# A fused attention and feed-forward block on one core: another opening, and other orders of work in the main loop

## Chip, core and metric

One core of a Trainium2 chip runs the whole program as one launch. The metric is the device time in microseconds (us), lower is better. The times of the kernel before are the median of three runs; the profile is of one further execution.

## What is computed

The input x has 4 sequences of 1024 tokens of width 256, all float32. The reference, cut to what matters:

```python
xn = layernorm(x)                                   # per token, over 256
q = rope(xn @ wq + bq) * 16 ** -0.5                 # 16 heads of 16
k = rope(xn @ wk + bk); v = xn @ wv + bv            # 2 groups of 16; 8 query heads share a group
attn = softmax(q @ k.T * 16 ** -0.5)                # per head, 1024 x 1024
att = (attn @ v).reshape(4, 1024, 256) @ wo + bo
hidden = silu(xn @ W1.T) * (xn @ W3.T)              # width 1024
hidden = fwht(hidden)                               # Walsh-Hadamard transform over 1024, / sqrt(1024)
out = x + att + hidden @ W2.T
```

The transform over `hidden` is put onto `W2` once, in the opening: a transform over 1024 is one over 8 (between chunks of 128) times one over 128 (within a chunk, a product with a 128x128 matrix `had`).

## The kernel before

**Blocks and iterations.** The 4096 tokens are 8 blocks of 512 (`NBLK`). There are 8 iterations (`NIT`), one for each sequence and group of heads. An iteration `i` computes the attention of 8 heads over a whole sequence, and in its gaps it prepares block `i + 2` and computes the feed-forward part of block `i`.

**Periods.** An iteration has 16 periods. Each has two steps `j`. A step has four score products on TensorE (`score`, L1374), four exponentials on ScalarE (L942) and one accumulation of exponentials times values (`sums`, L1387). Each period also holds four units `S1` of a first pass over the scores (L1297), whose maxima VectorE takes (`unit`, L1124); this pass runs 24 units ahead (`LEAD`), since the second pass subtracts the maxima inside its product.

**Fillers.** `main_entry` and `extra_entry` say what else a period holds: `XT` turns a normalised block (L1313), `QK` and `Q2` project queries, and keys and values (L1277), `VT` turns values, `MT` turns maxima (L1302), `WO` applies wo (L1307), `UP` makes one eighth of the hidden layer (L1339), `DN` applies W2 (L1352), `W2` does the 128-wide part of the transform of the weights (L1359). Before, iteration 0 has `XT`, `QK`, `W2`, `W2` in periods 0 to 3, then eight `UP` and four `DN`. Iterations 1 to 5 have `XT`, `QK`, `WO`, `WO`, eight `UP`, four `DN`. Iterations 6 and 7 have nothing in periods 0 and 1. A kind with an `MT` or `VT` beside it has an x behind its name (`UPx`).

**The ring.** All but the second-pass scores and the sums share two PSUM slots of two banks. `piece` waits until its slot has been emptied by ScalarE, VectorE or both. The order of the pieces on TensorE within a period is written out by hand for each kind in `walk_iteration`; `own` issues pieces of the filler, `first` an S1 unit, `scores` a pair of score products. ScalarE's, VectorE's and GpSimd's orders are written out by hand too, and each engine works strictly in its order.

**Second pass.** Its scores use three PSUM banks in turn: product `u` waits for exponential `u - 3`.

**The opening** (`walk_opening`) has two blocks: loads, statistics on VectorE, `root` (L805 to L811) on GpSimd, `normalise` (L886) on ScalarE, transposes, projections, rotation of queries (`rotate_queries`, L548 to L562) and keys (`rotate_keys`, L572 to L579), a way through HBM that changes the layout (`store_queries`, `store_keys`, `load_keys`, `load_queries`), and 24 S1 units. The 8-wide part of the transform of W2 is `transform`, three stages of two operations each (L526, L527), two stages on VectorE and one on GpSimd. `weights_lo` (L532) splits the first weights. Products of 32-bit values are made as three products of a high and a low part (`TERMS`), except the transposes, `WO`, `W2` and the sums, which are plain float32.

## Time and profile before

| what | value |
|---|---|
| median of 3 runs | 1179.03 us (1177.75 to 1181.44) |
| profiled execution, its own time | 1181.6 us |
| its span, first to last instruction | 1179.8 us |
| TensorE busy | 1049.8 us, 89% |
| VectorE, ScalarE, GpSimd busy | 783.2, 704.7, 352.2 us |
| mean granted TensorE clock | 0.936 of full speed |
| start of the first exponential | 100.90 us |

Views name the engines PE (TensorE), PEld (its weight loads), DVE (VectorE), ACT (ScalarE), POOL (GpSimd) and SP (SyncE); a q behind a name is the engine's queue, which issues DMAs. A row of the timeline has the start in us, the duration of the merged group, the engine, the line, the operation and its tiles, the count, and in brackets the idle time of the engine before it and what ended it.

### The profile page before, as it was taken

The numbers are of one execution on the slowest core, as the hardware profiler recorded it, in microseconds if no ns is written. First come the engines' busy times: TensorE is split into PE (matmuls) and PEld (weight loads), VectorE is DVE, ScalarE is ACT, GpSimd is POOL, SyncE is SP. The second block draws the span as 40 slices with busy tenths as digits, with TensorE's granted clock in tenths as the row PEclk, the third lists the DMA queues.
The fourth block names the chain that finished last, engine by engine and source line by source line (L and its number), as shares of the span: only waits on it lengthen the run. The fifth ranks groups of instructions, "written<-read, shape, count | busy, mean of one in ns | idle before, by whom it ended". The sixth has DMA issues, their size and how long they took to land.

```text
span 1179.8 us, 19333 instructions
## 1 busy us (share of the span) xinstructions
PE 1049.8 (89%) x7584; PEld 547.5 (46%) x7584; DVE 783.2 (66%) x891; ACT 704.7 (60%) x1318; POOL 352.2 (30%) x299
## 2 busy tenths in 40 slices
PE   0358899989998999989998999989999999999994
PEld 0314354544555455544555445554445344544552
DVE  4895477757776577766777577765777777687611
ACT  2204377656765477655775567754775667656771
POOL 1652523107330254106330164204440023102310
PEclk9755799989999899989999799989999999999997
DMA  8247022412314223412205123421204101410001
GB/s 222 67 150 192 21 67 68 101 59 72 89 31 88 70 82 88 94 63 75 83 13 109 54 99 89 88 69 31 73 20 101 48 24 46 95 36 6 7 17 51
DMA packets 62732, 84.27 MB, mean 71 GB/s; under 512 B 16688, under 2 KB 31920, under 8 KB 62640
## 3 DMA queue, kind: packets, MB, share of 16 engines
q1 hardware_dynamic: 59328, 78.30, 24.8%
q10 hardware_dynamic: 3312, 4.72, 1.6%
q8 instruction: 60, 0.98, 0.4%
q14 instruction: 32, 0.26, 0.1%
HBM read 55.18 MB, written 22.54 MB: 66 GB/s over the span
## 4 chain that ended last, share of the span: by engine, by line
PE 79%; DVE 12%; ACT 3%; issue 2%; ACTq 1%; SPq 1%; DMA 1%; POOL 0%; POOLq 0%; DVEq 0%
PE ps L1387 19%; PE ps L1339 16%; PE ps L1374 15%; PE ps L1297 13%; DVE negpart L1124 9%; PE ps L1352 7%; PE ps L1277 3%; PE ps L1307 3%; ACT work L942 2%; PE ps L1313 1%; ACTq L878 1%; DVE y L1106 1%; PE ps L1302 0%; DVE y L1104 0%; ACT osum L950 0%
## 5 line engine op out<-in xcount | busy, mean ns | idle before, releaser
L1124 DVE TENSOR_REDUCE negpart<-ps 128x2 f32<-128x1024 f32 x512 | 619.3, 1223 | 272.6 <-PE ps L1297 267.7
L942 ACT ACTIVATE work<-ps 128x512 f32<-128x512 f32 x1024 | 552.9, 605 | 266.4 <-PE ps L1374 211.0
L1297 PE MATMUL ps<-kb,qh 48*128 48x512 f32 x1024 | 257.7, 472 | 53.4 <-DVE negpart L1124 27.4
L1374 PE MATMUL ps<-qh,kb 50*128 50x512 f32 x1024 | 272.0, 470 | 20.0 <-ACT work L942 19.3
L1387 PE MATMUL ps<-work,vb 128*32 128x512 f32 x2048 | 282.0, 626 | 0.0
L1374 PEld LDWEIGHTS ps<-qh,kb 50*128 50x128 f32 x1024 | 121.2, 192 | 218.9 <-ACT work L942 166.8
L1339 PE MATMUL ps<-xf,w_p 64*128 64x512 f32 x1536 | 207.1, 401 | 5.9 <-DVE negpart L1124 3.5
L1297 PEld LDWEIGHTS ps<-kb,qh 48*128 48x128 f32 x1024 | 109.2, 197 | 149.0 <-DVE negpart L1124 83.2
L1339 PEld LDWEIGHTS ps<-xf,w_p 64*128 64x128 f32 x1536 | 140.7, 186 | 52.6 <-DVE hid L1096 12.7
L825 POOL TENSOR_TENSOR hid_p<-hid,hid_p 128x512 fp32r<-128x512 f32 x64 | 82.3, 1286 | 196.0 <-ACT hid_p L933 196.0
L831 POOL TENSOR_TENSOR attnt<-attnt,recips 128x512 f32<-128x512 f32 x16 | 20.4, 1278 | 374.6 <-DMA recips<-recip_rows 374.6
L821 POOL TENSOR_TENSOR hid<-hid 128x512 f32<-128x512 f32 x64 | 82.4, 1288 | 150.8 <-DVE hid L1096 147.5
L1352 PE MATMUL ps<-w2t_p,hid_p 64*128 64x256 f32 x1536 | 114.5, 279 | 0.0
L1352 PEld LDWEIGHTS ps<-w2t_p,hid_p 64*128 64x128 f32 x1536 | 110.1, 185 | 5.6 <-DVE negpart L1124 1.4
L1387 PEld LDWEIGHTS ps<-work,vb 128*32 128x32 f32 x2048 | 41.4, 109 | 83.1 <-issue 57.6
L921 ACT ACTIVATE hid<-ps 128x512 f32<-128x512 f32 x64 | 38.6, 603 | 42.5 <-PE ps L1339 41.0
L1104 DVE TENSOR_TENSOR y<-y,ps 128x256 f32<-128x256 f32 x32 | 13.4, 419 | 59.0 <-PE ps L1352 59.0
L1307 PE MATMUL ps<-wo_sb,attnt 128*128 128x256 f32 x128 | 40.6, 429 | 12.5 <-POOL attnt L831 12.5
L1096 DVE SCALAR_TENSOR_TENSOR hid<-hid,ps 128x512 f32<-128x512 f32 x64 | 43.4, 678 | 9.4 <-ACT hid L921 9.4
L886 ACT ACTIVATE xn<-xn,nmr,rstd 128x256 f32<-128x256 f32 x28 | 15.0, 596 | 43.7 <-POOL nmr L811 43.6
L933 ACT CAST hid_p<-hid 128x512 fp32r<-128x512 f32 x64 | 40.3, 630 | 0.0
L1277 PE MATMUL ps<-xt,wqkv_p 128*128 128x512 f32 x126 | 37.4, 446 | 1.6 <-ACT qe L908 0.9
(109 smaller groups left out, 489.0 us busy)
## 6 DMA issues: line engine op xcount, KB each, us to landing
xf<-xn_parts SPq DMA_DIRECT2D x32, 512.0 KB, 7.8
qh<-qk_parts SPq DMA_DIRECT2D x192, 64.0 KB, 2.2
xn_parts<-xt SPq DMA_DIRECT2D x14, 512.0 KB, 3.6
y<-in_x SPq DMA_DIRECT2D x8, 512.0 KB, 4.1
attnt<-osum SPq DMA_DIRECT2D x128, 32.0 KB, 2.0
recips<-recip_rows SPq DMA_DIRECT2D x128, 32.0 KB, 1.8
out<-y SPq DMA_DIRECT2D x8, 512.0 KB, 2.9
xn<-in_x SPq DMA_DIRECT2D x7, 512.0 KB, 4.5
```

The costliest lines, as they stand in the source:

```text
L821: nc.gpsimd.tensor_tensor(hid[1][:, c, :], hid[1][:, c, :], hid[0][:, c, :], ALU.mult).then_inc(hid_done, 1)
L825: nc.gpsimd.tensor_tensor(hid_p[1][:, c, :], hid[1][:, c, :], hid_p[0][:, c, :].bitcast(F32), ALU.subtract).then_inc(hid_lo, 1)
L942: nc.scalar.activation(prob[j % 2][:, h, :], ps[:, 4 + u % 3, :], ACT.Exp, scale=SCALE).then_inc(exp_done, 1)
L1096: nc.vector.scalar_tensor_tensor(at, at, 1.0, two(slot)[:, 0, :], ALU.add, ALU.mult).then_inc(ring_free[slot], 1)
L1124: nc.vector.tensor_reduce(negpart[a][:, f, :, h, t, e], two(slot), AX.X, ALU.max, negate=True).then_inc(ring_free[slot], 1)
L1277: m = pe.matmul(out, left[a], right[b], start=(first and n == 0), stop=(last and n == 2))
L1297: m = pe.matmul(bank[:, r, :], qh[2 * q + f][rows, h, t * P:(t + 1) * P], kb[i % 2][rows, e * 512:(e + 1) * 512], start=True, stop=True)
L1307: m = pe.matmul(bank[:, k // 2, k % 2 * D:(k % 2 + 1) * D], attnt[:, f, k * P:(k + 1) * P], wo_sb[:, i % NG, :], start=True, stop=True)
L1339: m = pe.matmul(bank[:, r, :], w13_p[w][rows, k, c * P:(c + 1) * P], xf[v][rows, k, :], start=(k == 0 and t == 0), stop=(done and t == 2))
L1352: m = pe.matmul(bank[:, r, 0:D], hid_p[w][rows, c, at * P:(at + 1) * P], w2t_p[v][rows, c, :], start=(c == 0 and t == 0), stop=(c == HC - ...
L1374: pe.matmul(ps[:, 4 + u % 3, :], kb[i % 2][rows, kt * P:(kt + 1) * P], qh[2 * a + f][rows, h, :], start=True, stop=True).then_inc(s2_done, 1)
L1387: m = pe.matmul(ps[VW * h:VW * (h + 1), 7, :], vb[b % 2][g][:, kt, :], prob[j % 2][:, h, :], start=(kt == 0), stop=(kt == ST - 1))
```

## The change

**Opening.** The first weights (`w13_raw`), `bo` and `wo` are no longer loaded from ScalarE's queue at the start, but from SyncE's after the queries of iteration 0. W2 and `had` are loaded from SyncE's queue. Six of VectorE's ten initial memsets go to GpSimd (two small zeros, four of ones in `kb`). ScalarE casts `wqkv` first, then normalises both blocks. TensorE's order is by kind, both blocks each: `XT`, `Q2`, `QK`, `VT`. VectorE rotates the keys of both blocks and then the queries of both; GpSimd rotates none. Keys are stored and loaded back from ScalarE's queue.

**W2.** Of the three stages of the 8-wide transform, one is left (on GpSimd). The other two and the 128-wide part are one accumulation on TensorE, `weights2`, 32 products of 128x128 by 128x256 in float32, between `VT` and the first S1 unit, in the four banks that the second pass uses later. The `W2` fillers are gone.

**Turned block.** Its evacuation is done in two halves (`turned_hi(m, k)`, `turned_lo(m, k)`).

**Placement.** Iteration 0 has nothing in periods 0 and 1, `XT` and `QK` in 2 and 3; the cast of the first weights (`weights_hi`) and the normalisation of block 2 stand on ScalarE at the end of periods 0 and 1, and `weights_lo` is all on GpSimd. In iterations 6 and 7 `WO` is in periods 0 and 4, `UP` in 1, 2, 3, 5, 6, 7, 8, 10, and 9 and 11 have no filler.

**Orders.** Nearly all hand-written orders within a period differ. The core of the diff:

```diff
+def turn_at(i):
+    return 0 if i > 0 else 2
+def sums_at(i):
+    return (2, 3) if i + 2 < NBLK else (0, 4)
+def up_at(i):
+    return range(4, 12) if i + 2 < NBLK else (1, 2, 3, 5, 6, 7, 8, 10)
...
+FULLS = {"XT": 2, "QK": 2}
+FREES = {"XT": 2, "UP": 2, "VT": 2}
...
         elif kind == "XT":
-            sums_before()
-            own(0)
-            first(1)
-            extra()
-            first(1)
-            scores(0)
-            own(1)
-            scores(1)
-            first(1)
-            scores(2)
-            first(0)
-            scores(3)
-            sums(i, 2 * p)
+            first(1)
+            own(0, 1)
+            scores(0)
+            scores(1)
+            sums_before()
+            extra()
+            first(0)
+            first(1)
+            scores(2)
+            scores(3)
+            first(0)
+            sums(i, 2 * p)
...
         elif kind == "UPx":
+            scores(0)
             first(0)
-            scores(0)
+            first(1)
             sums_before()
             scores(1)
-            first(1)
-            own(0, 1)
-            first(1)
-            own(2, 3)
-            first(1)
+            own(0)
             scores(2)
+            first(1)
+            own(1, 2)
+            first(1)
+            own(3)
...
         elif kind == "WO":
+            extra()
+            first(0)
+            first(0)
+            sums_before()
+            first(1)
+            scores(0)
+            scores(1)
+            own(0, 1, 2, 3)
...
-def walk_opening(piece):
-    for entry, slot in ((("XT", 0), 0), (("XT", 1), 1), (("QK", 0), 0), (("Q2", 0), 0), (("QK", 1), 1), (("Q2", 1), 0),
-                        (("VT", 0), 1), (("VT", 1), 0)):
-        for k in range(PIECES[entry[0]]):
-            piece(entry, k, slot)
+def walk_opening(piece, weights2):
+    for kind in ("XT", "Q2", "QK", "VT"):
+        for m in range(2):
+            for k in range(PIECES[kind]):
+                piece((kind, m), k, m)
+    weights2()
...
@@ SyncE @@
             load_tables(1)
+            sp.dma_start(w2h[0], w2t.rearrange("(c p) n -> p c n", p=P)).then_inc(w2_in, 16)
+            sp.dma_start(had, had_in).then_inc(w2_in, 16)
             swap_keys(0)
             swap_keys(1)
             store_queries(0)
-            store_keys(0)
-            store_keys(1)
-            load_keys(0)
             load_queries(0, 0, 0)
...
             place_maxima(0, 0, 0)
-            load_turned(0)
             load_queries(0, 1, 0)
             load_queries(0, 1, 1)
+            for n in range(2):
+                cols = slice(n * HID // 2, (n + 1) * HID // 2)
+                for r, src in enumerate((w1t, w3t)):
+                    sp.dma_start(w13_raw[GRP * r:GRP * (r + 1), :, cols],
+                                 src.rearrange("(c p) n -> p c n", p=GRP)[:, :, cols]).then_inc(w13_in[n], 16)
+            sp.dma_start(bo_sb[:, :], bo.partition_broadcast(P)).then_inc(bo_in, 16)
+            sp.dma_start(wo_sb[:, :, :], wo.rearrange("(g p) n -> p g n", p=P)).then_inc(wo_in, 16)
+            load_turned(0)
...
@@ GpSimd @@
             root(1)
-            rotate_keys(pool, nc.gpsimd, 0)
-            rotate_queries(pool, nc.gpsimd, 1)
-            weights_lo(pool, nc.gpsimd, 1)
-            transform(pool, nc.gpsimd, 1)
+            pool.wait_ge(w2_in, 32)
+            pairs = [t.rearrange("p (n s) d -> p n s d", s=2) for t in w2h]
+            for n, op in enumerate((ALU.add, ALU.subtract)):
+                nc.gpsimd.tensor_tensor(pairs[1][:, :, n, :], pairs[0][:, :, 0, :], pairs[0][:, :, 1, :],
+                                        op).then_inc(w2h_done, 1)
             root(2)
+            for n in range(2):
+                weights_lo(pool, nc.gpsimd, n)
...
@@ ScalarE, kinds UP and XT @@
                         exponentials(i, j, 1, 4)
+                        gate(i, up_at(i).index(p))
                         hidden_before(i, p)
-                        gate(i, p - 4)
                         exponentials(i, j, 4, 5)
-                        linear(i, p - 4)
+                        linear(i, up_at(i).index(p))
                         exponentials(i, j, 5, 8)
...
                     elif kind == "XT":
-                        turned_hi(i + 2)
+                        turned_hi(i + 2, 0)
+                        exponentials(i, j, 0, 1)
+                        turned_hi(i + 2, 1)
+                        exponentials(i, j, 1, 3)
                         save_finished(i, p)
-                        exponentials(i, j, 0, 8)
+                        exponentials(i, j, 3, 8)
...
@@ TensorE @@
+            def weights2():
+                pe.wait_ge(w2h_done, 2)
+                for o in range(HC):
+                    for c in range(o % 2, HC, 2):
+                        sign = bin(o // 2 & c // 2).count("1") % 2
+                        m = pe.matmul(ps[:, 4 + o // 2, o % 2 * D:(o % 2 + 1) * D], had[:, sign * P:(sign + 1) * P],
+                                      w2h[1][:, c, :], start=(c < 2), stop=(c >= HC - 2))
+                    if o % 4 == 3:
+                        m.then_inc(w2_full, 1)
```

## Rows read from the trace of the kernel before

**Rows 1.** The page's costliest groups: busy us, mean ns, idle before and its releaser.

```profile
L821 POOL TENSOR_TENSOR hid<-hid 128x512 f32<-128x512 f32 x64 | 82.4, 1288 | 150.8 <-DVE hid L1096 147.5
```

**Rows 2.** Windows, one per iteration (0, 1, 2): length, busy (count), clock, DMA.

```profile
100.90:246.80 145.90, 134.36 (x946) 69.94 (x946) 93.79 (x107) 88.96 (x167) 47.38 (x39) 0.91 0.27 74
246.80:380.80 134.00, 127.47 (x946) 66.76 (x946) 93.47 (x108) 87.31 (x166) 43.93 (x38) 0.97 0.28 71
380.80:517.10 136.30, 130.09 (x946) 67.86 (x946) 93.53 (x108) 87.26 (x166) 43.91 (x38) 0.95 0.28 77
```

**Rows 3.** The chain that ended last, within the opening: start, us, what.

```profile
7.92 9.03 ACTq L878
...
59.52 2.08 DMA qh<-qk_parts
...
62.51 18.20 DVE negpart L1124 x16
```

**Rows 4.** Loads issued in the first 30 us: count, KB, median us to landing.

```profile
hid<-in_w3t ACTq DMA_DIRECT2D x2, 512.0 KB, 15.1
...
xn<-in_x SPq DMA_DIRECT2D x1, 512.0 KB, 5.3
attnt<-in_x SPq DMA_DIRECT2D x1, 512.0 KB, 9.8
```

**Rows 5.** Timeline of the opening, all engines.

```profile
23.21 1.40 DVE L1071 BATCH_NORM_STATS2 stats<-attnt 128x6 f32<-128x256 f32 x4
...
27.00 2.07 ACT L886 ACTIVATE attnt<-attnt,nmr,rstd 128x256 f32<-128x256 f32 x4 [2.28 <-POOL nmr L811]
...
30.75 3.66 PE L1277 MATMUL ps<-xt,wqkv_p 128*128 128x512 f32 x12
...
37.79 0.69 DVE L552 TENSOR_TENSOR qe<-qe,tabq_sb 128x512 f32<-128x512 f32 x1
...
46.81 1.63 DVE L575 TENSOR_TENSOR hid<-hid 128x512 f32<-128x512 f32 x1
```

**Rows 6.** Timeline: eight instructions of four float32 products of 256 columns.

```profile
121.75 1.99 PE L1359 MATMUL ps<-y,osum 128*128 128x256 f32 x8
...
1171.28 3.75 PE L1307 MATMUL ps<-wo_sb,attnt 128*128 128x256 f32 x8 [12.51 <-POOL attnt L831]
```

**Rows 7.** Windows before and in stretches of lower clock; columns as in rows 2.

```profile
240.40:247.20 6.80, 4.10 (x31) 1.70 (x23) 4.70 (x5) 1.77 (x3) 0.00 (x0) 0.99 0.20 54
247.20:254.00 6.80, 6.51 (x25) 3.48 (x25) 3.55 (x4) 4.77 (x10) 0.00 (x0) 0.50 0.50 176
...
643.00:649.90 6.90, 5.43 (x45) 2.52 (x41) 4.43 (x5) 1.66 (x4) 0.00 (x0) 1.00 0.22 59
649.90:663.50 13.60, 12.08 (x41) 5.93 (x42) 7.17 (x6) 7.68 (x15) 0.00 (x0) 0.50 0.25 89
...
97.80:114.00 16.20, 15.32 (x51) 7.59 (x52) 8.39 (x7) 7.73 (x14) 4.69 (x2) 0.50 0.73 220
```

**Rows 8.** Timeline of iteration 1's period 0, which turns a block.

```profile
244.07 0.50 PE L1297 MATMUL ps<-kb,qh 48*128 48x512 f32 x2 [1.32 <-DVE negpart L1124]
...
245.43 1.01 ACT L896 CAST xt<-ps 128x1024 fp32r<-128x1024 f32 x1 [5.14 <-PE ps L1313]
...
247.49 0.79 PE L1374 MATMUL ps<-qh,kb 50*128 50x512 f32 x1 [1.67 <-ACT work L942]
```

**Rows 9.** Timeline of a plain UP period, iteration 1.

```profile
291.10 0.62 ACT L933 CAST hid_p<-hid 128x512 fp32r<-128x512 f32 x1
...
291.77 0.60 ACT L921 ACTIVATE hid<-ps 128x512 f32<-128x512 f32 x1
...
292.41 0.60 ACT L942 ACTIVATE work<-ps 128x512 f32<-128x512 f32 x1
```

**Rows 10.** Timeline around the first UP period of iteration 0.

```profile
142.53 2.93 PE L1339 MATMUL ps<-xf,w_p 64*128 64x512 f32 x12 [1.32 <-DVE negpart L1124]
...
146.24 1.93 PE L1387 MATMUL ps<-work,vb 128*32 128x512 f32 x8
```

More of the change, by code:

```diff
@@ L67, in extra_entry @@
 def extra_entry(i, p):
-    if p == 1 and i + 2 < NBLK:
+    if p == turn_at(i) + 1 and i + 2 < NBLK:
         return ("Q2", i + 2), 0
@@ L205, in walk_iteration @@
             scores(1)
+            sums_before()
             scores(2)
+            scores(3)
             first(1)
-            sums_before()
             own(0, 1, 2, 3)
             first(1)
-            scores(3)
+            sums(i, 2 * p)
             extra()
-            sums(i, 2 * p)
         elif kind is None:
@@ L269, in walk_iteration @@
             scores(3)
-        elif kind == "W2x":
+        elif kind == "XTx":
+            first(1)
+            own(0, 1)
+            scores(0)
+            scores(1)
+            sums_before()
+            first(0)
+            first(1)
+            scores(2)
+            scores(3)
+            first(0)
+            sums(i, 2 * p)
+            extra()
+        elif kind == "QKx":
             scores(0)
             first(1)
+            first(0)
+            scores(1)
             sums_before()
-            scores(1)
-            first(1)
-            own(0, 1)
             scores(2)
@@ L317, in skip @@
         pass
-    walk_opening(count)
+    walk_opening(count, skip)
     for i in range(NIT):
@@ L488, in build @@
         N_PARTS = 16 * 8
+        N_QUERIES = 16 * 4
         NORM = 4
@@ L1062, in _ @@
+                    if i == 0 and p < 2:
+                        normalise(2, range(2 * p, 2 * p + 2))
+                        weights_hi(p)
                     if p in (13, 14) and i + 3 < NBLK:
```

460 lines of the change are left out of this document (227 added, 233 removed).

## Prediction

> **What bounds the kernel now.** I read the table of busy times first: TensorE is busy for 89% of the span, far above the others. Then the windows, one per iteration: in iterations 1 and 2 TensorE is busy for 127.5 of 134.0 us and for 130.1 of 136.3 us, while VectorE has 93.5 and ScalarE 87.3 [rows 2]. So from iteration 1 on TensorE sets the pace, and an order within a period can give back only the 6 us or so per iteration in which it idles, and what its clock costs. These two iterations do the same work; the granted clock is 0.97 in the one and 0.95 in the other, which is one stretch of 6.8 us more at half clock (1.2 instead of 2.4 GHz), and that costs 136.3 - 134.0 = 2.3 us. Then the opening: its chain goes through a stalled DMA issue on ScalarE (9.03 us), projections, rotations, the way through HBM, and 1.14 us per S1 unit on VectorE (18.20 / 16) [rows 3]. The first exponential is at 100.90 us, and TensorE hardly works until then. This is where there is something to gain. The end isn't touched.
>
> **The opening, step by step.** The stalled issue goes, since ScalarE has four loads left. Block 1 is now the late one: it is the third issue of SyncE, near 1.8 us, and lands 9.8 us later [rows 4], at 11.6; bounds are 5.3 us (block 0's) and 9.8. Statistics to normalisation took 27.00 - 23.21 = 3.8 us, normalisation 2.07 [rows 5]: 17.5 us, where it was 29.1. Before, the statistics stood behind VectorE's low part of wqkv, and that behind ScalarE; block 0 is done in the meantime. Six memsets on GpSimd stand ahead of `root`: no row shows one. Below, the 0.9 us that VectorE took; above, twice that, as GpSimd's operations on 512 columns (1.29 us, [rows 1]) against VectorE's 0.69 [rows 5]. That is 6 to 12 us, and costs block 1 nothing, or 1.5 us.
> Transposes take 2 us (19.5). The projections take 3.66 / 12 = 0.31 us each [rows 5], so the keys of block 0 are out at 21.3; with an evacuation (one operation of 512 columns, 0.7) and the swap (two small DMAs, about 0.5 to issue and 2.1 to land like those of [rows 3]) VectorE turns to them at 24.6 (21.3 + 0.7 + 2.6). It has 2 x 5 operations on keys and 10 on block 0's queries before the store, 20 x 0.68 = 13.6 us: 38.2. The price is that of VectorE alone (0.69); with GpSimd at work beside it, it was 1.63 [rows 5]. Here GpSimd has only two operations of 1024 columns, over by then. Store: four issues of 0.46 and some 3 us; load: six of 0.46 and 2.1 [rows 3]: 9.7 us, hence 47.9. The keys go from ScalarE's queue beside that and are in by 41. The first reduction is at 48.9 instead of 62.5.
> From there 24 units at 1.14 us. Before, stage 2 of the transform, block 2's statistics and its transposition stood between unit 18 and the first exponential; now only the turned maxima (1.3 us). Last S1 product at 76.3, first exponential at 77.1 instead of 100.9.
>
> **W2 on TensorE.** 32 products of the form of L1359 are 64 instructions. Eight took 1.99 us at full clock and 3.75 at half [rows 6]: 64 x 0.233 = 14.9 us or 29. They start when `VT` is done: 19.5 + 36 projections at 0.25 to 0.31 = 30.7. At full clock they end at 45.6, before the queries land at 47.9, so they cost nothing; their cover is the rotation and the way through HBM. At half clock they end near 60, and all behind them is 12 us later. I take full clock: before, the clock had risen within the projections, and these now stand without a gap in front.
>
> **Iteration 0.** Period 0 has TensorE at half clock: before, it stayed there for 16.2 us while busy for 95% [rows 7]. Eight pairs of score and S1 products at 0.8 [rows 8] and two sums at 1.93 [rows 10] are 10.3 us. Period 1 lies between that and ScalarE's 8 x 0.60 [rows 9], plus 1.0 for half a normalisation and 1.9 for a cast of 2048 columns (1.01 for 1024, [rows 8]), 7.7: I take 9. `XT` takes 9 with its maxima and `QK` 10.8, as sums of their pieces at full clock. 76.3 + 39 + 0.7 = 116 for the first UP piece, where it was 142.5 [rows 10]: 26.5 us gained. Just after that point the old one was still at half clock (a sum in 1.93 us, [rows 10]), one stretch, 2.3 us. GpSimd rotates block 2's queries in front of its first product for UP, 10 operations of up to 1.29 [rows 1], which end about when ScalarE needs it: 1 us, bounds 0 and 3. Together 27.8.
> The first weights are issued near 78 and landed 15.1 us after issue in the old crowd [rows 4]; alone 7 or 8. ScalarE needs their first half near 87. I take no wait, bound 6 us, since ScalarE stands with all its exponentials behind that cast.
>
> **Iterations 1 to 5.** Turning a block leaves TensorE idle: 1.32 us for a reduction, 1.67 for an exponential held up while ScalarE waited 5.14 us for the second half [rows 8]. By halves and with both pieces first, I count 8.7 us where it was 9.8 apart from the clock: 1 us each, 5 in all. More depends on the clock. It falls right after that period, where TensorE had been busy for 4.10 of 6.8 us, in another iteration for 5.43 of 6.9 [rows 7]. I count 85% for the new order, so the fall should mostly go: eight stretches in five iterations at 2.0 (the first of each costs a little less than 2.3) are 16 us.
> The Trainium skill (TensorE: Matmul & The Clock Gate, the section on the HAM clock gate) says that the throttled clock is the default and that work releases it; the row agrees in that idling is followed by 0.50. By that rule the sum would gain these 16 us only if idling ends, and that isn't given.
>
> **What the new orders cost.** In UP periods ScalarE now makes the high part of hidden (0.62 us) between `gate` and the fifth exponential, where it filled a wait before: `gate` at 291.77, exponential at 292.41 [rows 9]. The exponential is up to 0.62 us later; TensorE needs it about 0.5 us after. So 0.1 us for 45 plain periods; in the 19 UPx, which now begin with scores, 0.4. That is 12 us, bounds 0 and 51 (0.62 in each plain one, twice that in UPx). In iterations 6 and 7 two `first(0)` in a row wait for a reduction; against the idle time of the old empty periods 1 us each: 2.
>
> **Sum.** -27.8 - 5 - 16 + 12 + 2 = -34.8. The sum is made on an execution of 1181.6 us (span 1179.8), 2.6 above the median of the runs; 1179.0 - 34.8 = 1144.
>
> **Rivals.** (a) The clock still falls after each turned block: 5.43 of 6.9 us was not enough, and 85% is my count. 1144 + 16 = 1160. (b) The opening stays slow: the products for W2 at half clock, since TensorE waits between its pieces until then; or the first weights late. 1144 + 12 = 1156. Against it is that the clock had risen within the old projections. The Trainium skill's rule (TensorE: Matmul & The Clock Gate, the section on the HAM clock gate) speaks for it. (c) More comes back: the new orders close most of the 6 us idle and cost nothing; 1144 - 12 - 6 = 1126. (d) Slower than before: the cast in front of the fifth exponential is not hidden. At its upper bound it costs 51 in place of 12: 1144 + 39 = 1183. It decides from (34.8 + 12) / 64 = 0.73 us per UP period. Against it: ScalarE idles for a third of an iteration, 134.0 - 87.3 us [rows 2]. (e) Nothing moves, since two of these cancel the opening.
>
> **Chances.** Forecast (1138 to 1150) 0.44; (a) 0.24; (b) 0.12; (c) 0.14; (d) 0.04; (e) 0.02. The range 1125 to 1162 takes in (a), (b) and (c) each by itself, but not (d), (e), or (a) and (b) together. About 0.3% is what a measurement can tell from no change. Faster 0.94, same 0.02, slower 0.04.
>
> **What would show it.** First exponential near 77 us and TensorE busy without a gap from 31 to 46 at full clock: if its products for W2 take 0.45 us each, (b). First UP product near 116. No stretch of 0.50 after a turned block from iteration 1 on: if there is, (a). UP periods as long as before: if they are longer, with TensorE idle before scores and ScalarE's exponential the releaser, (d). The prediction is wrong if TensorE's busy time per iteration grows, or if ScalarE waits for the first weights in periods 0 and 1.

## The result, and the profile after

The changed kernel takes 1146.78 us (median of four runs, 1145.47 to 1148.60), the kernel before 1179.0 in the same session: a ratio of 0.9714, 95% interval 0.9695 to 0.9733. The prediction was 1144, range 1125 to 1162. The profiled execution took 1145.47 us, its span is 1143.9. Three executions in the experiments were far slower than all others of their kernel (3068.1 us in the first kernel of experiment 3, 1393.8 in experiment 5, 1864.0 in experiment 7); medians and ratios here leave them out.

The windows of iterations 0, 1, 2, 6 and 7, each from its first exponential to the next one's, of the kernel after (columns as in [rows 2]):

```profile
75.33:212.81 137.48, 131.47 (x933) 69.08 (x933) 95.18 (x116) 92.05 (x172) 58.01 (x45) 0.90 0.46 115
212.81:342.87 130.06, 125.99 (x947) 66.41 (x946) 93.69 (x109) 86.51 (x166) 43.81 (x38) 1.00 0.28 73
342.87:472.90 130.03, 125.97 (x947) 66.41 (x946) 93.67 (x109) 86.51 (x165) 43.81 (x38) 1.00 0.31 81
...
866.12:995.42 129.30, 119.83 (x917) 62.56 (x916) 90.56 (x96) 81.96 (x157) 22.90 (x18) 0.99 0.21 50
995.42:1119.80 124.38, 117.70 (x847) 62.10 (x850) 58.46 (x66) 81.32 (x155) 22.89 (x18) 0.91 0.04 11
```

The same two windows of the kernel before:

```profile
917.26:1041.43 124.17, 118.86 (x918) 60.80 (x916) 90.55 (x97) 82.18 (x156) 23.12 (x18) 1.00 0.21 52
1041.43:1155.20 113.77, 110.23 (x861) 57.00 (x863) 61.62 (x69) 81.43 (x156) 23.14 (x18) 1.00 0.06 14
```

Iterations 1 and 2 took 134.0 and 136.3 us at a clock of 0.97 and 0.95 [rows 2]; now both take 130.0 at 1.00, with TensorE idle for 4.1 us instead of 6.2 to 6.5. Iterations 6 and 7 have become longer, by 5.1 and 10.6 us, though they do the same work: the change lost 15.7 us there.

**The opening.** TensorE's timeline, kernel after:

```profile
16.97 1.97 PE L1368 MATMUL ps<-ident,attnt 128*128 128x128 f32 x8 [2.49 <-ACT attnt L922]
18.81 2.18 PE L1330 MATMUL ps<-xt,wqkv_p 128*128 128x512 f32 x6
...
28.77 0.43 PE L1383 MATMUL ps<-ident,hid 32*128 32x32 f32 x4 [0.42 <-ACT hid L945]
29.13 14.08 PE L1419 MATMUL ps<-y,osum 128*128 128x256 f32 x64
46.72 0.74 PE L1350 MATMUL ps<-kb,qh 48*128 48x512 f32 x4 [3.51 <-issue]
```

VectorE's timeline in the same stretch, kernel after:

```profile
24.45 0.69 DVE L593 TENSOR_TENSOR kh<-kv,tabk_sb 128x512 f32<-128x512 f32 x1 [4.16 <-DMA kr<-kv]
...
42.30 0.69 DVE L582 TENSOR_TENSOR hid<-hid,attnt 128x512 fp32r<-128x512 f32 x1
...
43.44 2.35 DVE L1223 TENSOR_TENSOR w2t_p<-ps,w2t_p 128x1024 fp32r<-128x1024 f32 x2
47.26 18.20 DVE L1180 TENSOR_REDUCE negpart<-ps 128x2 f32<-128x1024 f32 x16 [1.48 <-PE ps L1350]
```

And the first exponential, from ScalarE's timeline:

```profile
75.33 2.86 ACT L980 ACTIVATE work<-ps 128x512 f32<-128x512 f32 x5 [31.07 <-PE ps L1436]
```

The 64 instructions for W2 stand without a gap from 29.13 to 43.21, 0.22 us each, and end 3.5 us before the S1 unit that waits for the queries. The rotation costs 0.69 us an operation on all of VectorE's list. The first reduction is at 47.26 (62.51 before, [rows 3]) and takes the same 18.20 us for 16.

**The turned block.** TensorE, ScalarE and VectorE about period 0 of iteration 1, timeline of the kernel after, to be held beside [rows 8]:

```profile
211.25 1.09 PE L1368 MATMUL ps<-ident,xn 128*128 128x128 f32 x8
...
211.94 0.59 ACT L932 CAST xt<-ps 128x512 fp32r<-128x512 f32 x1 [1.71 <-PE ps L1368]
...
212.81 0.60 ACT L980 ACTIVATE work<-ps 128x512 f32<-128x512 f32 x1 [0.28 <-PE ps L1436]
213.30 0.58 ACT L932 CAST xt<-ps 128x512 fp32r<-128x512 f32 x1
213.46 0.50 PE L1436 MATMUL ps<-qh,kb 50*128 50x512 f32 x1 [0.46 <-ACT work L980]
```

Its windows, 6.8 us each (columns as in [rows 2]):

```profile
205.00:211.80 6.80, 6.80 (x77) 5.15 (x74) 4.61 (x6) 4.20 (x9) 1.30 (x1) 1.00 0.20 47
211.80:218.60 6.80, 6.03 (x37) 2.35 (x37) 5.32 (x6) 5.70 (x11) 0.00 (x0) 1.00 0.15 36
```

TensorE idles for 0.46 us in one piece where it idled for 1.32 and 1.67; it is busy for 6.03 of 6.8 us, and the clock stays at 1.00 [rows 7: 4.10 of 6.8, then 0.50]. (That the busier stretch is why the clock stays is not shown; see experiment 2.)

**Where the 35.9 us of the span came from**, as sums between first exponentials over the two traces (XT is the period that turns a block; the wait for it falls into period 15 before it, since that ends with the first exponential behind the turning):

| part | before | after | difference | predicted |
|---|---|---|---|---|
| opening, to the first exponential | 100.90 | 75.33 | -25.6 | -23.8 |
| iteration 0, periods 0 to 14 | 132.04 | 129.64 | -2.4 | -4.0 |
| period 15 of iterations 0 to 4 | 69.41 | 39.18 | -30.2 | -21 (five of order, 16 of clock), with the next |
| periods 0, 1 of iterations 1 to 5 | 89.49 | 83.24 | -6.2 | |
| periods 2, 3 (WOx) of iterations 1 to 5 | 88.76 | 95.30 | +6.5 | 0 |
| periods 4 to 11 (UP) of iterations 1 to 5 | 303.78 | 307.76 | +4.0 | +12, for all iterations |
| periods 12 to 14 of iterations 1 to 5 | 124.43 | 124.85 | +0.4 | 0 |
| period 15 of iteration 5, iterations 6 and 7 | 246.36 | 264.51 | +18.1 | +2 |
| closing | 24.60 | 24.05 | -0.5 | 0 |

The sum came out near the forecast by luck, because its terms were wrong against each other: period 15 and the two periods behind it gave 15 us more than I counted for the turned block, and the last iterations cost 16 us more; the 6.5 us of WOx, which no term has, stand against UP periods that cost less than the 12.

Period 15 can be cut once more, at its last exponential (sums over iterations 0 to 4, in us). "Within" is from its first exponential to the end of its last; "wait" is from there to the first exponential of the next iteration, which stands behind the turning:

| kernel | within | wait |
|---|---|---|
| before | 36.8 | 32.7 |
| after | 26.3 | 12.9 |
| after, old order of XT (experiment 1) | 26.3 | 31.4 |
| before, new order of XT (experiment 2) | 36.8 | 20.8 |

So 10.5 of the 30.2 us do not belong to the turned block at all: they come with the other new orders, whether XT is new or old. The new order of XT alone takes 11.8 us off the wait; the other parts, the two halves among them, take 7.9 us more off it, but only 1.3 without that order.

### The profile page after: what moved, and what is told of

Same layout as the page of the kernel before. It is cut to its first block, busy times and chain, and to the rows that moved or that the text cites. A ratio compares the mean times of both kernels' runs of the same rounds, so it can differ in the third digit from the quotient of the medians.

```text
span 1143.9 us, 19466 instructions
## 1 busy us (share of the span) xinstructions
PE 1054.3 (92%) x7632; PEld 560.1 (49%) x7632; DVE 772.9 (68%) x903; ACT 701.2 (61%) x1326; POOL 335.9 (29%) x291
## 4 chain that ended last, share of the span: by engine, by line
PE 77%; DVE 10%; ACT 6%; issue 3%; DMA 2%; SPq 1%; POOL 0%; POOLq 0%; DVEq 0%; ACTq 0%
PE ps L1451 19%; PE ps L1395 16%; PE ps L1436 16%; PE ps L1350 12%; PE ps L1407 8%; DVE negpart L1180 6%; ACT work L980 4%; PE ps L1362 3%; PE ps L1330 3%; PE ps L1368 1%; ACT hid_p L971 1%; DMA hid<-in_w3t 1%; DVE y L1162 1%; ACT hid L967 1%; DVE y L1219 1%
## 5 line engine op out<-in xcount | busy, mean ns | idle before, releaser
L1436 PE MATMUL ps<-qh,kb 50*128 50x512 f32 x1024 | 283.5, 463 | 21.2 <-ACT work L980 21.2
L1350 PE MATMUL ps<-kb,qh 48*128 48x512 f32 x1024 | 260.7, 465 | 32.5 <-DVE negpart L1180 24.1
L1451 PE MATMUL ps<-work,vb 128*32 128x512 f32 x2048 | 278.8, 617 | 0.0
L1436 PEld LDWEIGHTS ps<-qh,kb 50*128 50x128 f32 x1024 | 127.2, 189 | 221.7 <-ACT work L980 166.3
L1395 PEld LDWEIGHTS ps<-xf,w_p 64*128 64x128 f32 x1536 | 144.7, 185 | 35.1 <-DVE hid L1152 7.0
L1219 DVE TENSOR_TENSOR y<-y,ps 128x1024 f32<-128x1024 f32 x16 | 19.5, 1221 | 38.2 <-PE ps L1362 38.2
L1362 PEld LDWEIGHTS ps<-wo_sb,attnt 128*128 128x128 f32 x128 | 25.9, 219 | 26.2 <-issue 19.3
L967 ACT COPY hid<-ps 128x512 f32<-128x512 f32 x64 | 37.4, 585 | 0.0
```

What stands on the lines that cost most here:

```text
L967: nc.scalar.copy(hid[0][:, c, :], two(slot)[:, 1, :]).then_inc(ring_free[slot], 1)
L1350: m = pe.matmul(bank[:, r, :], qh[2 * q + f][rows, h, t * P:(t + 1) * P], kb[i % 2][rows, e * 512:(e + 1) * 512], start=True, stop=True)
L1362: m = pe.matmul(bank[:, k // 2, k % 2 * D:(k % 2 + 1) * D], attnt[:, f, k * P:(k + 1) * P], wo_sb[:, i % NG, :], start=True, stop=True)
L1395: m = pe.matmul(bank[:, r, :], w13_p[w][rows, k, c * P:(c + 1) * P], xf[v][rows, k, :], start=(k == 0 and t == 0), stop=(done and t == 2))
L1436: pe.matmul(ps[:, 4 + u % 3, :], kb[i % 2][rows, kt * P:(kt + 1) * P], qh[2 * a + f][rows, h, :], start=True, stop=True).then_inc(s2_done, 1)
L1451: m = pe.matmul(ps[VW * h:VW * (h + 1), 7, :], vb[b % 2][g][:, kt, :], prob[j % 2][:, h, :], start=(kt == 0), stop=(kt == ST - 1))
```

## The experiments

Times are medians; ratios are to the kernel before, with 95% intervals. The clock makes executions of one kernel differ by one or two stretches, up to 2.5 us each (below), and the kernel before took 1178.9 to 1181.7 us from session to session, so periods are read from the trace and not from the total where the effect is small.

**1. The turned block, undone.** In the changed kernel, the kind XT alone goes back to the old order on three engines (VectorE's part is left out below; the evacuation stays in two halves):

```diff
-            first(1)
-            own(0, 1)
-            scores(0)
-            scores(1)
-            sums_before()
-            extra()
-            first(0)
-            first(1)
-            scores(2)
-            scores(3)
-            first(0)
+            sums_before()
+            own(0)
+            first(1)
+            extra()
+            first(1)
+            scores(0)
+            own(1)
+            scores(1)
+            first(1)
+            scores(2)
+            first(0)
+            scores(3)
...
-                        exponentials(i, j, 0, 1)
                         turned_hi(i + 2, 1)
-                        exponentials(i, j, 1, 3)
                         save_finished(i, p)
-                        exponentials(i, j, 3, 8)
+                        exponentials(i, j, 0, 8)
```

> The changed kernel with the old order of the period that turns a block (kind XT, iterations 1 to 5) on all three engines; the halves stay. If most of what iterations 1 to 5 gained comes from the clock that no longer falls, its stretches of 0.50 return and the kernel takes 1164 to 1168. If it is the order alone, about 1 us for each of five, 1152 and no stretch of 0.50.

Measured: 1179.78 us, ratio 0.9998 (0.9982 to 1.0015). In this kernel the one order, in five of 128 periods, is worth 33 us, as much as the whole change. Its windows before the clock falls, after it, and iteration 1:

```profile
208.10:214.90 6.80, 5.48 (x55) 3.15 (x51) 3.69 (x6) 2.71 (x5) 0.89 (x1) 1.00 0.23 62
214.90:232.00 17.10, 15.90 (x53) 8.06 (x52) 8.43 (x8) 7.79 (x15) 0.00 (x0) 0.50 0.20 70
217.13:354.05 136.92, 131.28 (x946) 69.54 (x946) 93.29 (x109) 86.48 (x166) 43.70 (x38) 0.95 0.26 69
```

TensorE had been busy for 5.48 of 6.8 us when the clock fell; 6.03 of 6.8 had kept it (experiment 2 has a counterexample). The loss splits in two: period 15 of iterations 0 to 4 is 18.5 us longer (57.65 against 39.18, mostly TensorE waiting for the slot and the reduction), periods 0 and 1 of iterations 1 to 5 are 15.3 us longer (98.49 against 83.24, half clock). It also shows what is not of this order: period 15 is still 11.8 us shorter than before (57.65 against 69.41), 10.5 of it within the period and 1.3 in the wait (table above). The 10.5 come from other new orders, the next suspects being those of the DN periods; I tried none of them alone.

**2. The turned block alone.** The kernel before, with the new order of XT on the three engines, its evacuation still in one piece of 1024 columns:

```diff
                         turned_hi(i + 2)
+                        exponentials(i, j, 0, 3)
                         save_finished(i, p)
-                        exponentials(i, j, 0, 8)
+                        exponentials(i, j, 3, 8)
...
-                        units(i, u, 2)
+                        units(i, u, 1)
+                        extra_before(i, p)
                         turned_lo(i + 2)
-                        extra_before(i, p)
-                        units(i, u + 2, 2)
+                        units(i, u + 1, 3)
```

> The kernel before, with one edit: the period that turns a block (period 0 of iterations 0 to 5) gets the changed order on TensorE, ScalarE and VectorE (one S1 unit, both pieces of the turned block, then scores; three exponentials before the finished sums are stored), while its evacuation stays in one operation of 1024 columns. All else, the opening, the cast behind the gate and the last iterations, is as before. Theory, that this order alone keeps TensorE's clock up: iterations 1 to 6 of the kernel before had 54.7 us at half clock, at 0.385 us each 21 us, and the order itself is 1 us shorter in each: 1179.7 - 21 - 5 = 1154, with hardly a stretch at half clock in iterations 1 to 5. Rival 1, that it takes the halves too (with them together ScalarE and VectorE empty the slot later, TensorE idles on): 1174 to 1180. Rival 2, that the clock holds only with TensorE's work around it as the other new orders have it: a part of the stretches is left, about 1165.

Measured: 1162.63 us, ratio 0.9843 (0.9811 to 0.9876). Windows of its iterations 1 and 2, the one stretch of lower clock in iterations 1 to 5, and the stretch about the turning in iteration 1:

```profile
242.27:373.54 131.27, 125.69 (x946) 65.11 (x946) 93.33 (x107) 87.27 (x166) 43.96 (x38) 1.00 0.27 72
373.54:504.77 131.23, 125.65 (x946) 65.09 (x946) 93.34 (x107) 87.25 (x165) 43.94 (x38) 1.00 0.29 80
...
767.30:777.50 10.20, 9.25 (x35) 3.55 (x35) 5.12 (x5) 5.53 (x12) 0.00 (x0) 0.50 0.26 91
...
238.80:245.60 6.80, 4.59 (x28) 2.16 (x28) 4.10 (x4) 3.60 (x7) 0.00 (x0) 1.00 0.14 40
```

All iterations 1 to 4 run at full clock, so the theory holds in kind: the order alone does it, without the halves. In size it was 8.6 us short of the forecast (1154), and the second rival's number (1165) is nearer. 3.2 us of the 17.5 between the two spans are not even the edit's: they lie in the opening (first exponential at 97.67 for 100.90), which it does not touch. Two reasons stand in the periods. First, with the old order a stretch at half clock right behind the turned block costs almost nothing. Period 1 takes 10.24 us here without any, and took 10.53 and 10.25 before in iterations 1 and 3, with one; where there were two it took 12.72 to 12.88. So the first is worth at most 0.3 us and the second 2.5 (estimates: period 1 stands behind another order in each case). (Not so with the new order: in iteration 5 here all of period 0 is at half clock, and it takes 9.42 us for 6.04.) Second, that fall in iteration 5 was left, and another in iteration 6. Period 15 of iterations 0 to 4 takes 57.6 us together, 11.8 less than before, all of it in the wait.

The last row shown is of the turning in iteration 1: TensorE was busy for only 4.59 of 6.8 us, and the clock stayed at 1.00. In the changed kernel it fell in iteration 3 behind this stretch, with no idle piece longer than 0.46 us:

```profile
494.50:501.30 6.80, 5.90 (x34) 2.25 (x27) 4.62 (x7) 4.24 (x8) 6.25 (x5) 1.00 0.06 14
```

So neither the busy time of such a stretch nor its longest idle piece tells whether the clock falls. That the order keeps the clock up is shown by the edit; by what, is not.

**3. The last iterations: placement and order.** Three kernels. The first takes the changed kernel and puts WO back into periods 2 and 3 and UP into 4 to 11 of iterations 6 and 7:

```diff
-    return (2, 3) if i + 2 < NBLK else (0, 4)
+    return (2, 3)
...
-    return range(4, 12) if i + 2 < NBLK else (1, 2, 3, 5, 6, 7, 8, 10)
+    return range(4, 12)
```

> The changed kernel with WO in periods 2 and 3 and UP in 4 to 11 of iterations 6 and 7 too, as before; all else as changed. Those two iterations took 237.9 us before (917.26 to 1155.2, first exponential to last) and 253.7 after (866.12 to 1119.8), 15.8 more. If the placement itself is the cause, with its four WO periods outside any filler-free neighbourhood, they return to about 240 and the kernel to 1133. If the new order of the kind WO (two first(0) in a row) is the cause, it is met only twice instead of four times here, and the kernel comes to 1139. If neither, 1147.

The second leaves the placement and gives the kind WO its old order on three engines (on TensorE):

```diff
-            extra()
-            first(0)
+            scores(0)
+            first(1)
+            extra()
             first(0)
-            sums_before()
-            first(1)
-            scores(0)
             scores(1)
-            own(0, 1, 2, 3)
+            sums_before()
             scores(2)
             sums(i, 2 * p)
+            own(0, 1)
             first(1)
             scores(3)
+            own(2, 3)
+            first(1)
```

> The changed kernel with the old order of the kind WO on all three engines, and the new placement kept. Each WO period in the trace idles TensorE for 1.03 to 2.04 us before a second first(0), and the granted clock falls after some of them. If this order is the cause of the loss in iterations 6 and 7, they come near 240 us and the kernel to 1134; if the placement is, it stays within 3 us of 1147.

The third does both, and a third thing: in iterations 6 and 7 it gives WOx its old order on TensorE too:

> As e1_place, and in iterations 6 and 7 both WO periods also have the orders of before (WOx and WO). e1_place still spent 14.57 and 13.78 us in period 2 of those iterations where before had 9.07, with 10.2 and 6.8 us at half clock. If the WO orders after two empty periods are what lets the clock fall, period 2 returns to 9.1, iterations 6 and 7 together to 240 us, and the kernel takes 1131. If the clock falls by chance of its timing against these periods, the sum stays at 248 us and the kernel at 1138.

Measured, with iterations 6 and 7 from the traces:

| kernel | median us | ratio (95%) | iteration 6 | iteration 7 |
|---|---|---|---|---|
| before | 1179.0 | 1 | 124.2 | 113.8 |
| after | 1146.8 | 0.9714 (0.9695 to 0.9733) | 129.3 | 124.4 |
| old placement | 1136.9 | 0.9653 (0.9621 to 0.9686) | 128.7 | 119.5 |
| old order of WO | 1143.6 | 0.9699 (0.9673 to 0.9725) | 129.9 | 120.8 |
| both, and old WOx order | 1133.7 | 0.9604 (0.9579 to 0.9628) | 122.7 | 116.3 |

By the medians the old placement alone gives back 9.8 us (7 by the ratios), the old order of WO alone 3.2, which the intervals do not tell from nothing, and the third kernel 13 us of 1146.8. The traces, one of each, show more where the clock elsewhere does not blur it: from period 15 of iteration 5 to the last exponential the changed kernel takes 264.5 us, and these 255.2, 257.8 and 246.1, so 9.3, 6.7 and 18.4 less. The parts roughly add up. The new order in the old place makes period 2 take 14.6 and 13.8 us (9.07 before). Most of that is WO's, though WO stands in period 3: it begins with two `first(0)`, so the scores for its first exponential come late. From the seventh exponential of period 2 to the first of period 3 it takes 4.44 and 5.25 us, and 0.97 in the third kernel; what lies before that, WOx, takes 2.5 us more than there in the two iterations. The old order in the new place makes periods 0 and 4 of iteration 6 take 11.3 and 14.1. What goes wrong in the changed kernel is seen on TensorE's timeline about its iteration 6:

```profile
863.93 0.50 PE L1350 MATMUL ps<-kb,qh 48*128 48x512 f32 x2 [1.32 <-DVE negpart L1180]
864.36 1.07 PE L1451 MATMUL ps<-work,vb 128*32 128x512 f32 x8
...
867.20 2.00 PE L1362 MATMUL ps<-wo_sb,attnt 128*128 128x256 f32 x8
...
871.65 0.49 PE L1350 MATMUL ps<-kb,qh 48*128 48x512 f32 x2 [1.03 <-DVE negpart L1180]
```

and in the windows of TensorE's half clock in its iterations 6 and 7:

```profile
992.80:999.60 6.80, 6.54 (x21) 3.39 (x14) 1.06 (x1) 2.66 (x5) 0.00 (x0) 0.50 0.10 23
1030.40:1037.20 6.80, 6.54 (x18) 3.63 (x14) 0.67 (x1) 3.16 (x6) 1.27 (x1) 0.50 0.08 21
1088.40:1098.60 10.20, 9.94 (x53) 4.85 (x54) 0.00 (x0) 5.54 (x12) 1.27 (x1) 0.50 0.04 9
```

Two S1 units in a row in the same slot wait for a reduction of 1.22 us, which I priced at 1 us each. The products for wo then also stand in one block of 2 us in which neither VectorE nor ScalarE gets anything from TensorE; whether this block or the two units cost the 6.7 us is not shown, since the second kernel undoes both. And the clock falls three times, 24 us at half where there were none before: two falls are just ahead of the WO periods 0 and 4 of iteration 7, the third is in its periods 11 and 12, and no run shows why.

**4. The cast behind or ahead of the gate.** In the plain UP periods the high part of hidden is made ahead of the gate again:

```diff
-                        gate(i, up_at(i).index(p))
                         hidden_before(i, p)
+                        gate(i, up_at(i).index(p))
                         exponentials(i, j, 4, 5)
```

> The changed kernel with ScalarE's cast of hidden before gate again in plain UP periods (45 of them). If the cast in front of the fifth exponential costs 0.1 us each, as the prediction has it, 1142; if it is hidden, 1147; if the eight UP periods of an iteration are 0.75 us longer than before for this alone, 1141.

> e5_last with ScalarE's cast of hidden ahead of gate in plain UP periods. In the trace of e4_cast an iteration of this kind was 0.3 us shorter than in the changed kernel, so 2 us less than e5_last: 1129 by the first theory there. If that cast is hidden, the same time as e5_last.

The first is on the changed kernel: 1146.74 us, ratio 0.9720 (0.9697 to 0.9743), no different. The second is on top of the last of experiment 3: 1126.27 us, 0.9543 (0.9526 to 0.9561), 7.4 us less than without. The trace says 0.3 us per iteration in both (129.74 against 130.03 in iterations at full clock: three UP periods take 6.12 instead of 6.47, two UPx 10.0 instead of 9.8, period 12 8.39 instead of 8.16), 2.4 us in eight, if the others gain as much. The profiled executions of the two kernels with the old last iterations differ by 3.9 us of span, with 51 and 42 us at half clock in their iterations. What the rest of the 7.4 us is, these runs do not settle: executions of the two with nearly the same mean granted clock (0.965 and 0.964) are still 5 us apart (1130.6 and 1131.2 against 1125.9 and 1126.0), so the amount of half clock alone does not explain it.

**5. WOx.** The periods 2 and 3 of iterations 1 to 5, which no term of the prediction has, get their old order too, on top of the kernel of 1126.3 (TensorE's and ScalarE's lists):

```diff
-            own(0)
-            scores(1)
-            scores(2)
-            first(1)
-            own(1, 2, 3)
-            first(1)
+            own(0)
+            scores(1)
+            own(1)
+            first(1)
+            scores(2)
+            own(2, 3)
+            first(1)
             sums_before()
...
-                        exponentials(i, j, 0, 7)
+                        exponentials(i, j, 0, 1)
                         save_finished(i, p)
-                        exponentials(i, j, 7, 8)
+                        exponentials(i, j, 1, 8)
```

> On top of the kernel with the old orders and places in the last two iterations and the high part of hidden made before the gate (1126.3 us), periods 2 and 3 of iterations 1 to 5 get their old order of TensorE and ScalarE too (products for wo one by one between the scores, finished sums stored after the first exponential). These two periods took 18.79 us an iteration in the changed kernel and 17.75 in the kernel before. Theory, that this comes from the order within the two periods: 17.75 again, so 5 x 1.04 = 5.2 us less, 1121. Rival 1, that the two periods are longer because of what the new order of the period that turns a block leaves to them: 18.8 as now, 1126. Rival 2, that the old order leaves TensorE idle for longer and its clock falls in more stretches: one stretch of 3.4 us at half clock costs 1.3 us, and with two of them in each iteration the gain is gone, 1126 to 1134.

Measured: 1120.1 us, ratio 0.9494 (0.9475 to 0.9513), 6.2 us less. Its trace is of one further execution of the same kernel:

> The same kernel as the last but one (old order of periods 2 and 3 on top of the version with the old last iterations and the cast before the gate), for its trace: its time was 1120.4 us, and its profile was of an execution at a lower clock throughout. Theory: periods 2 and 3 of iterations 1 to 5 take 17.75 us an iteration instead of 18.79. Rival: they still take 18.8, and the 5.8 us came from elsewhere, by less time at half clock.

1119.39 us. Windows of its iterations 1, 2, 6 and 7:

```profile
213.13:341.83 128.70, 125.37 (x947) 65.69 (x946) 93.62 (x109) 86.91 (x166) 43.97 (x38) 1.00 0.28 74
341.83:470.53 128.70, 125.36 (x947) 65.69 (x946) 93.63 (x109) 86.91 (x166) 43.98 (x38) 1.00 0.30 82
854.62:977.02 122.40, 118.26 (x918) 61.17 (x916) 90.61 (x96) 82.05 (x157) 23.15 (x18) 1.00 0.22 53
977.02:1093.79 116.77, 113.43 (x861) 58.13 (x863) 61.20 (x68) 81.44 (x156) 23.12 (x18) 0.97 0.06 14
```

Iterations 1 to 4 take 128.70 us each, 1.0 less than with the new WOx order (129.7); periods 2 and 3 together 17.78 instead of 18.79. That is 5 us in five iterations; besides, the clock does not fall there in this trace, as it does once to three times in periods 2 and 3 in the traces of the kernels with the new WOx order. TensorE idles for 3.3 us per iteration instead of 4.1. This kernel, the change less four of its parts, is 27 us faster than the change and 60 us faster than before.

**6. How much cover the products for W2 have.** Each is made twice into the same sums (W2 comes out doubled, all other work is the same):

```diff
                 for o in range(HC):
-                    for c in range(o % 2, HC, 2):
+                    for k in range(2):
+                        for c in range(o % 2, HC, 2):
```

> Every product of the weights' transform is made twice on TensorE (64 products, so 128 instructions, in place of 64), into the same sums: W2 comes out doubled, which changes the output but no other work. In the changed kernel these 64 instructions took 14.08 us (29.13 to 43.21) at full clock, and the queries of iteration 0 landed at 46.63. Theory, that the first 14.1 us are free because they lie under the rotation and the way through HBM, and only what goes beyond that cover costs: 14.1 us more end at 57.3, the first reduction is at about 58 instead of 47.3 and the first exponential near 86 instead of 75.3; 1146.8 + 10.7 = 1157. Rival 1, that they are free however many there are, since something else holds the first reduction: 1147. Rival 2, that TensorE, now busy without a pause from 16 us into the first pass over the scores, keeps its full clock longer, and iteration 0 gives back a part: half clock for 3 to 4 stretches of 6.8 us less, at 0.385 us for each us at half clock some 8 to 10 us, hence 1148 to 1150. The three differ in the first exponential (86, 75, 86) and in the time at half clock in iteration 0 (27, 27, under 10).

Measured: 1159.88 us, ratio 0.9810 (0.9761 to 0.9858). Timelines of TensorE and VectorE:

```profile
29.62 27.89 PE L1420 MATMUL ps<-y,osum 128*128 128x256 f32 x128
57.44 0.73 PE L1350 MATMUL ps<-kb,qh 48*128 48x512 f32 x4
...
58.59 1.22 DVE L1223 TENSOR_TENSOR w2t_p<-ps,w2t_p 128x1024 fp32r<-128x1024 f32 x1 [12.59 <-ACT w2t_p L992]
59.73 18.18 DVE L1180 TENSOR_REDUCE negpart<-ps 128x2 f32<-128x1024 f32 x16
```

The first exponential is at 87.80, 12.5 us later, for 13.8 us of added products: the cover is gone after 3.5 us, and the late half of W2 puts its own evacuation of 1.22 us in front of the first reduction, which I had not counted. The second rival is out for the profiled execution (1163.08 us): the clock fell at 62.3 us, 5 us behind the products (after them by 4 us in the changed kernel too), and iteration 0 had 36 us at half clock, not under 10. The four executions lie far apart, though (1150.9 to 1165.1), and the fastest has the highest mean granted clock, 0.967 against 0.953; where it gained that, no trace shows.

**7. The large loads early.** The four loads of the first weights are issued from ScalarE's queue at the start, as they were:

```diff
             act.dma_start(tabq_sb[:, :, :], tabq[0]).then_inc(tabs_in, 16)
+            for n in range(2):
+                cols = slice(n * HID // 2, (n + 1) * HID // 2)
+                for r, src in enumerate((w1t, w3t)):
+                    act.dma_start(w13_raw[GRP * r:GRP * (r + 1), :, cols],
+                                  src.rearrange("(c p) n -> p c n", p=GRP)[:, :, cols]).then_inc(w13_in[n], 16)
```

> The changed kernel with the four loads of the first weights (2 MB) issued from ScalarE's queue at the start again. If the place of these loads in time carries the opening's gain, because they crowd block 1's and W2's loads, the first exponential comes 5 to 9 us later than 75.3 and the kernel takes 1152 to 1156. If only the stalled issue of the tenth DMA on ScalarE's queue cost time before, the first exponential is within 1.5 us of 75.3 and the kernel at 1147.

Measured: 1152.1 us, ratio 0.9766 (0.9742 to 0.9789), 5.3 us more by the medians (6 by the ratios). Its first exponential is at 81.05. Two timelines show how, VectorE's and GpSimd's:

```profile
26.87 2.21 DVE L593 TENSOR_TENSOR kh<-kv,tabk_sb 128x512 f32<-128x512 f32 x1 [4.88 <-DMA kr<-kv]
29.00 2.87 DVE L594 TENSOR_TENSOR kr<-kr,tabk_sb 128x512 f32<-128x512 f32 x1
...
26.13 5.19 POOL L875 TENSOR_TENSOR y<-work 128x1024 f32<-128x1024 f32 x2 [9.61 <-DMA osum<-in_had_in]
```

Block 1 lands 2 us later (12.74 against 10.78). And W2, issued at 3.89, lands at 25.6 instead of 15.1, so that GpSimd's two operations of 1024 columns no longer lie before the rotation but beside its first two operations, which take 5.1 us instead of 1.4. These two make the 5.7 us.

**8. GpSimd beside VectorE.** The rotation of block 1's queries goes to GpSimd:

```diff
-            rotate_queries(dve, nc.vector, 1)
...
+            rotate_queries(pool, nc.gpsimd, 1)
             root(2)
```

> The changed kernel with block 1's queries rotated on GpSimd again, beside VectorE's rotation of block 0's. If the two engines hinder each other as before (1.63 us for an operation of 0.69), block 0's queries are stored 5 to 7 us later and the first exponential is at 80 to 82, the kernel at 1152. If they don't, VectorE is done as before, GpSimd in 12 us, and the first exponential stays at 75 to 76.

Measured: 1155.63 us, ratio 0.9792 (0.9769 to 0.9814), 8.9 us more. VectorE's and GpSimd's timelines:

```profile
33.53 1.75 DVE L568 TENSOR_TENSOR xn<-qe,tabq_sb 128x512 f32<-128x512 f32 x1
35.20 1.75 DVE L569 TENSOR_TENSOR xn<-qe,tabq_sb 128x512 f32<-128x512 f32 x1
...
34.69 1.72 POOL L572 TENSOR_TENSOR hid<-hid,y 128x512 f32<-128x512 f32 x1
```

The operations of 0.69 us on VectorE take 1.09 to 1.75 while GpSimd runs, and GpSimd's take up to 1.72 for 1.29. Block 0's queries, which the first unit needs, are ready 9.6 us later (46.5 against 36.9), 0.9 of which was there before GpSimd began. A helper engine made the engine with the critical list slower than doing both alone, which was over at 43.0. The Trainium skill (SBUF — State Buffer, the section on the two separate sides) says that the two engines share a port pair by an exclusive lock when VectorE reads two operands from SBUF, and the GpSimd instruction reads it too, and that the one that comes second blocks until the first is done. The trace agrees in that both engines' operations are longer side by side. It does not show one waiting in full for the other: an estimate by that rule, one operation of each in turn, is 0.69 + 1.29 = 1.98 us, and the longest here took 1.75 and 1.72.

## Why the prediction was right, and where its steps were not

- **Opening.** Right in its steps, within 2.4 us each: block 1 landed at 10.78 (11.6 forecast), keys' rotation at 24.45 (24.6), products for W2 0.22 us each from 29.13 to 43.21 (30.7 to 45.6), queries landed at 46.6 (47.9), first reduction 47.26 (48.9), first exponential 75.33 (77.1). The unknown memset took 0.99 us for 32 rows of 1024 on GpSimd, as the lower bound, and ended at 5.8, ahead of `root`. Experiments 7 and 8 show that the two conditions I named (loads out of the way, GpSimd silent beside the rotation) matter, 5.7 and 8.5 us of first exponential out of 25.6.
- **W2 at full clock.** Right; rival (b) is out. Its margin was the 3.5 us of experiment 6. The weights for iteration 0 were never waited for (0.16 us).
- **Iteration 0.** First UP product at 117.98, forecast 116. Periods 0 to 14 gave 2.4 us for 4.
- **Turned block: both terms mis-sized, and a term missing.** I had 5 us of order and 16 of clock, 21; the periods gave 36.4. The wait for the turned block gave 19.8 (32.7 to 12.9), not 5: I compared 1.1 us of TensorE's idle time and didn't follow how ScalarE's first exponential moves when both transposes come first (ScalarE waits for a transpose for 5.14 us before, 3.25 with the order alone, 1.71 with all). The clock does stay up (rival (a) is out; experiment 1 shows what falls would have cost), but was worth about 8.1 us, not 16: periods 0 and 1 of iterations 1 to 5 took 89.5 us, and at full clock, with the new XT alone, take 16.28 in one iteration (experiment 2), 81.4 in five. I priced the first stretch of each fall like the second, and in the old order it costs 0.3 us at most. The changed kernel takes 83.2 there, 1.9 more, since its period 1 (QK, in a new order too) takes 10.61 for 10.24. The remaining 10.5 us, within period 15, come from other new orders, which no term has.
- **UP: half the size, and its split wrong.** Bounds 0 and 51, taken 12: UP periods cost 0.8 us per iteration, an estimate of 6 for eight. Of the plain ones, periods 5, 9 and 11 take 6.47 us for 6.13 and the others as long as before, 0.17 on average where I had 0.1. The UPx, where I had 0.4 each, take 9.75 and 9.79 for 9.76 and 10.08: they cost nothing. The cast behind the gate is 0.35 in each of the three plain periods, but with it the UPx and period 12 are 0.2 shorter each, so it costs 0.3 per iteration (experiment 4). Rival (d) needed 0.73 us per period.
- **WOx: a step that is missing.** The diff changed these orders and no term has them; they cost 5.2 us (experiment 5), and period 3 of iteration 3 is 1.4 longer with its 3.4 us at half clock.
- **Iterations 6 and 7: the term that failed.** Two `first(0)` in a row at 1 us each against the idle time of empty periods, +2; measured +18.1. The waits were of the forecast size (1.32, 1.03). But the term counted only them, and undoing the order of WO gives back 6.7 us, undoing the placement alone 9.3 (experiment 3). The two empty periods had cost little (5.57 and 5.68 us); with WO in period 0, the first exponential of iterations 6 and 7 comes later in the period before (10.80 and 11.94 us for 8.42), and period 0 itself takes 8.15 and 9.84 for 5.57. And the clock comes down, 24 us at half, which at 0.4 us for each (below) is an estimate of 10 us of the 18. With the placement and the orders of WO and WOx undone these stretches take 7.1, 122.7 and 116.3 us, 18.4 less (experiment 3).
- **Rival (c)** gave 1126 if the new orders cost nothing. They did cost. That the kernel without those of WO, the cast and the last placement takes 1126.3 is a coincidence, since other terms were off too; without WOx it is 1120.

Left open: which of the new orders gives the 10.5 us within period 15; what makes the clock fall or stay; and why total times fell by more than the cast's 0.3 us per iteration in experiment 4.

## What to carry to other kernels

A period that stalls the busiest engine for 1 or 2 us can be paid more than once: in its own wait, in the period before it and in the clock after it. So a rewritten schedule is to be judged period by period over the whole run, the last iterations too, since here undoing one order cost 33 us and the last iterations lost 18 unseen in the sum. Moved work is free only within its measured cover (here 3.5 us were left), and a helper engine beside the critical one can slow it (here by 9 us). When a large diff pays, undo its parts: here four of them together, the last placement, the orders of WO and WOx and the place of the cast, were a loss of 27 us, and the medians do not show each of them as one alone.

## What the runs showed of the hardware that was not expected

- TensorE's granted clock fell behind 6.8 us in which TensorE was busy for 4.10, 5.43, 5.48 and 5.90 us, with no idle piece longer than 1.67 us (0.46 in the last), and it kept its level with 6.03, but also with 4.59. Neither number sorts the cases.
- A us at half clock costs a full iteration 0.37 to 0.43 us (iteration 0: 137.5 us with 26.6 at half, 142.9 with 41.1; iteration 7: 113.9 with none, 116.8 with 6.8). Behind the turned block it cost at most 0.05 in the old order (0.3 us for the first 6.8, experiment 2), and 0.36 in the new one (period 0 at half clock 9.42 us for 6.04).
- A VectorE operation on 512 columns took 0.69 us alone and 1.09 to 2.87 us with GpSimd beside it.
